# A state-space block on one core: GpSimd makes the scan inputs two units at a time, one 128x1024 instruction in place of two of 128x512

## The reference, cut to what matters

```
x = x + 0.5 * ffn(layernorm(x))          # FFN "G": gate, up, 2:4 sparsify, down
x = x + mamba(layernorm(x))              # "M": the part that the change touches
x = x + 0.5 * ffn(layernorm(x))          # FFN "F"

# mamba: B = 8 sequences, L = 512 steps, E = 1024 channels, N = 16 states
u     = silu(causal_conv(xn @ W_in.T))
delta = softplus(u @ Wd1.T @ Wd2.T + bd2)
Bt, Ct = u @ WB.T, u @ WC.T                       # one row of L values per state n
def step(h, inps):
    h   = exp(d_l[..., None] * A) * h + (d_l * u_l)[..., None] * b_l[:, None, :]
    y_l = einsum('ben,bn->be', h, c_l)
out = ((y + u * W_D) * silu(xn @ W_skip.T)) @ W_out.T
```

## Time and profile before

| | |
|---|---|
| median of three runs | 3607.23 us |
| span of the profiled execution, first to last instruction | 3600.7 us |
| TensorE (PE) busy | 3360.2 us, 93% |
| VectorE (DVE) busy | 3027.7 us, 84% |
| GpSimd (POOL) busy | 2594.9 us, 72% |
| ScalarE (ACT) busy | 2061.7 us, 57% |

### The profile page before, as it was taken

The page is one execution under the profiler, slowest core; times in us unless marked ns, Lnnn a source line. Parts: engine busy times, 40 slices in busy tenths (PEclk is TensorE's granted clock), DMA queues, the critical chain, the costliest instruction groups (busy, mean ns, idle before and its releaser), DMA issues. The chain is left out here.

```text
span 3600.7 us, 39012 instructions
## 1 busy us (share of the span) xinstructions
PE 3360.2 (93%) x11958; PEld 2122.7 (59%) x12020; DVE 3027.7 (84%) x3597; ACT 2061.7 (57%) x2805; POOL 2594.9 (72%) x1625
## 2 busy tenths in 40 slices
PE   8999999999999999999999999988989889988899
PEld 6775566556655665566555565555545555555467
DVE  5546998788999889988898899988998988999934
ACT  5546657567565765566565675565555566454422
POOL 1316876667877779768787678868888878979913
PEclk9999999999999999999999999999999989999999
DMA  9656566657756676566665675647646556645433
GB/s 356 219 188 192 176 207 222 205 176 221 215 175 210 202 227 200 171 203 208 187 205 176 202 230 169 221 138 215 222 124 210 172 178 220 187 149 184 139 120 114
DMA packets 243470, 696.45 MB, mean 193 GB/s; under 512 B 23536, under 2 KB 23792, under 8 KB 233584
## 3 DMA queue, kind: packets, MB, share of 16 engines
q1 hardware_dynamic: 173632, 559.72, 45.1%
q10 hardware_dynamic: 69632, 134.23, 15.6%
HBM read 619.94 MB, written 76.55 MB: 193 GB/s over the span
## 5 line engine op out<-in xcount | busy, mean ns | idle before, releaser
L1381 POOL TENSOR_TENSOR scan_in<-du,scan_rows 128x512 f32<-128x512 f32 x1024 | 1312.8, 1294 | 700.9 <-DVE decay L1255 612.1
L1255 DVE TENSOR_TENSOR_SCAN decay<-decay,scan_in 128x512 f32<-128x512 f32 x1024 | 1252.4, 1223 | 157.0 <-ACT decay L865 150.9
L865 ACT ACTIVATE decay<-delta,small 128x512 f32<-128x512 f32 x1024 | 699.4, 689 | 935.4 <-DVE scan_out L1265 928.7
L1394 POOL TENSOR_TENSOR y<-y,scan_out 128x1024 f32<-128x1024 f32 x512 | 1227.0, 2397 | 0.6 <-DVE scan_out L1265 0.6
L637 PE MATMUL main<-zhi,wunit 128*128 128x512 f32 x2048 | 909.9, 444 | 62.1 <-DVE cmp L1195 38.3
L729 PE MATMUL side<-h,wdown 128*128 128x512 f32 x1760 | 801.8, 599 | 24.2 <-ACT sq L988 12.6
L639 PE MATMUL main<-zhi,wunit 128*128 128x512 f32 x2048 | 817.7, 399 | 0.0
L638 PE MATMUL main<-zlo,wunit 128*128 128x512 f32 x2048 | 816.7, 399 | 0.0
L1265 DVE TENSOR_TENSOR scan_out<-decay,scan_rows 128x512 f32<-128x512 f32 x1024 | 702.9, 686 | 27.6 <-POOL y L1394 2.2
L729 PEld LDWEIGHTS side<-h,wdown 128*128 128x128 f32 x1760 | 334.5, 191 | 392.7 <-issue 350.2
L637 PEld LDWEIGHTS main<-zhi,wunit 128*128 128x128 f32 x2048 | 390.2, 191 | 233.6 <-issue 89.5
(11 more groups left out here) (117 smaller groups left out, 3192.8 us busy)
## 6 DMA issues: line engine op xcount, KB each, us to landing
wunit<-hl_dram SPq DMA_DIRECT2D x480, 512.0 KB, 4.3
scan_rows<-bc_dram ACTq DMA_DIRECT2D x256, 512.0 KB, 5.7
wdown<-down_w_dram SPq DMA_DIRECT2D x256, 256.0 KB, 3.2
wmam<-mam_dram SPq DMA_DIRECT2D x128, 512.0 KB, 4.1
hl_dram<-wunit SPq DMA_DIRECT2D x32, 512.0 KB, 4.6
skip_dram<-skb SPq DMA_DIRECT2D x64, 256.0 KB, 4.2
delta<-skip_dram SPq DMA_DIRECT2D x16, 1024.0 KB, 6.7
wmam<-wout_dram SPq DMA_DIRECT2D x32, 512.0 KB, 4.3
```

Source lines behind the costliest of these rows:

```text
L865: nc.scalar.activation(decay[u % BANKS][:], delta[:, e, :], ACT.Exp, scale=aneg[:, e * N + n:e * N + n + 1]).then_inc(sem["decay_ready"], 1)
L1255: nc.vector.tensor_tensor_scan(decay[u % BANKS][:], decay[u % BANKS][:], db[u % INPUTS][:], 0.0, ALU.mult, ALU.add).then_inc(sem["state_re ...
L1381: nc.gpsimd.tensor_tensor(db[u % INPUTS][:], du[:, e, :], rows[m % ROWS][:, 0, :], ALU.mult).then_inc(sem["input_ready"], 1)
L1394: nc.gpsimd.tensor_tensor(y[:, e:e + 2, :], y[:, e:e + 2, :], scan_out[:, k:k + 2, :], ALU.add).then_inc(sem["sum_ready"], 1)
```

## The change

One `scan_input` call now makes the inputs of two units, u and u + 1 with u even. Its output is two neighbouring slots of `scan_in`, its first input two neighbouring blocks of `du`, and its second input the row of B, read twice by a dimension of two with step zero. The wait that frees the slots now asks for the scans of both units four earlier. `input_ready` counts pairs, and its four waiters are changed to fit. Nothing in the loops of the other engines is moved.

```diff
@@ sp: the two loads into du
-                        sp.wait_ge(sem["input_ready"], UNITS * (b + 1))
+                        sp.wait_ge(sem["input_ready"], UNITS * (b + 1) // 2)
...
-                        sp.wait_ge(sem["input_ready"], UNITS * b + HALF)
+                        sp.wait_ge(sem["input_ready"], (UNITS * b + HALF) // 2)
@@ dve: scan
-                dve.wait_ge(sem["input_ready"], u + 1)
+                dve.wait_ge(sem["input_ready"], u // 2 + 1)
@@ pool: scan_input
                 if u >= INPUTS:
-                    pool.wait_ge(sem["state_ready"], u - INPUTS + 1)
-                nc.gpsimd.tensor_tensor(db[u % INPUTS][:], du[:, e, :], rows[m % ROWS][:, 0, :], ALU.mult).then_inc(sem["input_ready"], 1)
+                    pool.wait_ge(sem["state_ready"], u - INPUTS + 2)
+                k = u % INPUTS
+                nc.gpsimd.tensor_tensor(scan_in[:, k:k + 2, :], du[:, e:e + 2, :], rows[m % ROWS][:, 0:1, :].broadcast_to([P, 2, L]),
+                                        ALU.mult).then_inc(sem["input_ready"], 1)
@@ pool: the loop over ticks
                 for u in plan.units_at[tick]:
-                    scan_input(u)
-                    if u % 2 == 1:
+                    if u % 2 == 0:
+                        scan_input(u)
+                    else:
                         if u // 2 >= LAG:
                             sum_states(u // 2 - LAG)
```

## The result

The changed kernel takes 3627.44 us (median of 5 runs, 3624.37 to 3629.29), the kernel before 3606.55 us (median of 5). The ratio is 1.0059 with a 95% interval of 1.0047 to 1.0071: 21 us slower (17 to 26). I had forecast 3611 us, a range that ended at 3625, and given "slower" 0.25. The forecast was wrong. In the experiments the kernel before was measured anew beside each set: 3605.31 us for experiments 1 to 4, 3604.45 us for 5 to 8, 3605.18 us for 9 to 12, and every ratio and difference is against that. One execution of the kernel before took 14751.5 us and one of experiment 8 took 6949.77 us; neither is counted here.

What follows compares the result with a forecast made beforehand. TensorE was taken to bound the kernel to 2300 us, with VectorE near the bound in the last third. Terms -1 + 1 + 1 + 3 = +4 us on 3600.7 make 3605; runs lie 6.5 higher: about 3611 us, range 3597 to 3625.

Steps and rivals of the forecast that it cites:

- The price of the new instruction: GpSimd's paired input costs 2.31 us by start-to-start spacing, like a sum of that width; repeating the row of B is free.
- GpSimd's time: GpSimd is busy 70 to 100 us less, which becomes waiting for scans; worth 0 to -4.1 us on the path, taken as -1.
- The first unit: The first scan needs a pair instead of one input and starts 1.1 us later; priced 0 to 1.1, taken as +1 us.
- The ring: Both inputs of a pair wait for scan 2p-3, so an input may reach VectorE late; 0 to +4 us, taken as +1.
- The waits for sums: VectorE's waits for GpSimd's sums, 2.2 and 1.9 us before, shrink slightly as sums come 0.14 us sooner; taken as -1 us.
- The loads into du: DMA loads wait for a half's last pair, ending at most 1.1 us later; values not needed until the next half; 0.
- An arrival at a random moment meets an instruction of length d in proportion to d, and waits d/2: VectorE instructions with two SBUF tensors wait for GpSimd's current instruction; 35.9 us excess grows by factor 1.28, +10 us on VectorE.
- I put a third on the path: Of the +10 us of longer waiting on VectorE, only a third reaches the end, +3 us, as TensorE covers the earlier stretches.
- slower by the longer holds: Rival, chance 0.17: all +10 us of VectorE waiting out longer GpSimd instructions reaches the end; +11 to +15, say 3620 us.
- Faster: Rival, chance 0.11: GpSimd's fewer, longer pauses let VectorE meet it idle more often; -10 or so, 3597 us.
- slow operand: Rival, chance 0.08: the repeated row of B makes GpSimd's input slow, 3.0 us per pair; +20 to +40, say 3637 us.
- The clock: TensorE's granted clock, averaging 0.95 from 2300 to 3420 us, adds noise: a shift of work could move 6 us either way.

Runs made afterwards that it cites:

- experiment 8: Kernel before with an added wait: the sum of pair p-3 waits for scan 2p-2, so even scans release the sum; 3615.14 us, ratio 1.0032.
- experiment 11: Changed kernel with GpSimd waiting until each group of VectorE instructions with two SBUF tensors is done before starting what the last scan released; 3588.55 us, ratio 0.9948.
- experiments 1 and 2: Kernel before: 1, first single input of each pair waits one scan longer, 3639.27 us; 2, each 128x1024 sum made as two 128x512 instructions, 3612.38 us.
- experiments 5 and 11: Changed kernel: 5, sum of pair p-3 also waits for scan 2p-2 except the last three of a half, 3608.68 us; 11, as under experiment 11, 3588.55 us.

## Why the prediction was wrong

*The price of the new instruction* (2.31 us by spacing, the repeat free): right. *GpSimd's time* (70 to 100 us less, turned into waiting): right, 76 us less, and 105 us more waiting. *The first unit* (+1.1): right, 1.0 us. *The ring* (+1): right in kind, VectorE never waits for an input later on; experiment 11 agrees. *The waits for sums*, forecast to fall by 1 us, rose by 5.9 (4.2 + 5.8 against 2.2 + 1.9). *The loads into du* (0): nothing in the trace speaks against it, and no run tested it alone.

*"An arrival at a random moment meets an instruction of length d in proportion to d, and waits d/2"*: this is the step that failed. The arrivals are not random. Both engines' programs are tied together by the scans: GpSimd is released by the end of a scan, and VectorE reaches most of its two-SBUF groups 0.6 to 3.6 us after the last scan (45 of 56, the median 2.2 us in both kernels). What a group then meets is set by how much work the scan released and how soon the group comes, and the change turned 3.54 and 1.23 us into 4.62 us and nothing. By lengths alone I got a factor of 1.28 and +10 us; experiments 1 and 2 show that lengths are not the cause, and experiments 5 and 11 that the release is. Measured: +17.4 us, a factor of 1.44. I had written down the very wait that did it ("now both wait for scan 2p-3"), and priced it only as a risk of a late input.

*"I put a third on the path"*: wrong as well. I took the busy shares to mean that TensorE covers VectorE's delays up to 2300 us. The gates' dates show the delay growing all along. A likely reason is that a TensorE that is busy 96% of a stretch still depends on VectorE emptying its banks just in time. No run tests that by itself: TensorE's waits for the FFN's low part rose only from 21.8 to 26.7 us. In the runs that moved the time by more than 15 us, 0.7 to 1.15 of each us on VectorE came back as time. With 17.4 + 6.9 us at 0.9, the price and the share known only afterwards, the sum would have been +22.

The rival "slower by the longer holds" (0.17, 3620 us) named the right resource and ranked too low; the rival's remark that the pair starts later and meets a gate more often was the mechanism itself. "Faster" and "slow operand" are out. The clock fell from 0.979 to 0.975 between the two profiled executions, but at an equal clock 20 us remain. What lowers it, and how much of TensorE's 13 us of longer busy time it makes up, stays open.

## What to carry to other kernels

Before two short instructions are merged on an engine that shares something with another, ask what releases them: a merged instruction starts at the later of the two releases, and its work lands in one piece behind it. Price instructions that exclude each other by their place after a common release, not by average busy shares, and look at two or three such places in both engines' timelines. When two engines collide at known points, let the one with idle time wait for the other: here that was worth 17 to 18 us, more than any change of shape.

## What the runs showed of the hardware

- VectorE instructions with two SBUF tensors and GpSimd instructions that read SBUF took turns one instruction at a time where they met: a gate of four, undisturbed 2.49 us, took 6.28 us beside two GpSimd instructions of 2.4 us that were ready together.
- GpSimd's memsets held up nobody: with 1025 us of them in the run, the same gate instructions took 685 ns.
- On GpSimd a 128x1024 product whose second operand repeats 512 columns by a step of zero took 2381 ns, a sum of two plain operands 2411 ns.
